# Retention in a two-layer language-model tower: on TensorE a tile's transposes are issued ahead of the scores of the tile four later

## What is computed

```python
gammas = 1.0 - exp(linspace(log(1/32), log(1/128), H))            # H = 8 heads of DH = 16
Dmat = gammas[:, None, None] ** abs(n[:, None] - n[None, :])      # 1024 x 1024 for each head
Q = _xpos(einsum('bsd,hde->bhse', X, W_Q), False)
K = _xpos(einsum('bsd,hde->bhse', X, W_K), True)
V = einsum('bsd,hde->bhse', X, W_V)
scores = einsum('bhse,bhte->bhst', Q, K)
p = softmax(scores, axis=-1) * Dmat[None]
Y = einsum('bhst,bhte->bhse', p, V)
...                                       # group norm of Y, gate with silu(X @ W_G)
return swish * Yn @ W_O
```

## Time and profile before

| | us |
|---|---|
| median of three executions | 3473.49 |
| lowest and highest of them | 3467.41 to 3475.9 |
| the profiled execution, its own time | 3499.97 |
| span of its profile | 3498.2 |
| first to last start of a tile's exponentials in it | 196.4 to 677.2 |

### The profile page before, as it was taken

One profiled execution on the slowest core, in us unless ns is written; L12 is line 12 of the kernel. 1 busy time (PEld: TensorE's weight loads), 2 busy tenths in 40 slices (PEclk: granted clock), 3 DMA queues, 4 the chain that ended last, 5 costly groups with the idle time before them and its releaser, 6 DMA issues.

```text
span 3498.2 us, 57433 instructions
## 1 busy us (share of the span) xinstructions
PE 3053.3 (87%) x18996; PEld 2673.3 (76%) x19032; DVE 2413.0 (69%) x4368; ACT 1801.3 (51%) x3135; POOL 1773.0 (51%) x1524
## 2 busy tenths in 40 slices
PE   1556666668999999879999999999799999999997
PEld 1434445457788888759999999999699999999986
DVE  1456766643677676657777777777577777777774
ACT  0256666523666565525555555555455555555544
POOL 5466656500200000126666666666366666666663
PEclk9879999969999999979999999999899999999997
DMA  1010000000000000010000000000000000000010
GB/s 41 32 25 18 19 13 18 7 25 21 13 0 0 0 0 0 11 50 28 27 27 27 27 27 27 27 27 28 17 28 27 27 27 27 27 27 27 27 34 7
DMA packets 36972, 75.92 MB, mean 22 GB/s; under 512 B 9644, under 2 KB 13876, under 8 KB 36120
## 3 DMA queue, kind: packets, MB, share of 16 engines
q1 hardware_dynamic: 35352, 71.68, 6.5%
q0 software_dynamic: 1536, 3.15, 0.3%
HBM read 65.36 MB, written 1.05 MB: 19 GB/s over the span
## 4 chain that ended last, share of the span: by engine, by line
PE 47%; issue 5%; POOL 3%; DVE 1%; ACT 0%; POOLq 0%; DVEq 0%; ACTq 0%
PE lat_ps_h L1837 19%; PE lat_ps_z L1851 9%; PE lat_ps_s L1763 7%; PE lat_ps_t L1790 6%; PE lat_ps_z L1781 3%; POOL lat_zz L1570 2%; PE lat_ps_z L1773 2%; PE lat_ps_z L1861 1%; POOL latm_wq L1549 0%; POOL latm_wq L1543 0%; POOL latm_att L1562 0%; POOL latm_vcg L1554 0%; PE lat_ps_s L1879 0%; DVE latm_norm L1669 0%; DVE latm_h L1675 0%
## 5 line engine op out<-in xcount | busy, mean ns | idle before, releaser
L1837 PE MATMUL lat_ps_h<-latm_share,latm_attT 100*128 100x256 f32 x6144 | 886.8, 286 | 0.1
L1837 PEld LDWEIGHTS lat_ps_h<-latm_share,latm_attT 100*128 100x128 f32 x6144 | 818.7, 189 | 24.9 <-DVE latm_attT L1626 11.8
L1562 POOL TENSOR_TENSOR latm_att<-latm_sc,latm_tot 128x400 f32<-128x400 f32 x516 | 441.3, 855 | 617.7 <-DVE latm_tot L1621 588.1
L1570 POOL TENSOR_TENSOR lat_zz<-lat_zz,lat_zsq 128x512 f32<-128x512 f32 x514 | 660.3, 1285 | 0.3
L1698 ACT ACTIVATE latm_sc<-latm_sc 128x400 f32<-128x400 f32 x516 | 279.1, 541 | 430.8 <-DVE latm_sc L1612 430.8
L1851 PE MATMUL lat_ps_z<-latm_attT,latm_vg 100*128 100x512 f32 x1536 | 485.8, 424 | 0.0
L1619 DVE TENSOR_REDUCE latm_tot<-latm_sc 128x4 f32<-128x400 f32 x516 | 291.3, 565 | 157.4 <-ACT latm_sc L1698 157.4
L533 POOL TENSOR_TENSOR ret_probs<-ret_probs,ret_shared 128x1024 f32<-128x1024 f32 x128 | 305.7, 2389 | 181.4 <-ACT ret_probs L666 181.4
L1626 DVE TENSOR_TENSOR latm_attT<-lat_ps_t,latm_attT 100x512 fp32r<-100x512 f32 x514 | 349.8, 681 | 61.7 <-ACT latm_attT L1714 61.7
L1714 ACT CAST latm_attT<-lat_ps_t 100x512 fp32r<-100x512 f32 x514 | 301.0, 586 | 147.3 <-PE lat_ps_t L1790 123.1
L1763 PE MATMUL lat_ps_s<-latm_wk,lat_xr 128*128 128x400 f32 x1548 | 368.8, 347 | 3.0 <-issue 3.0
(11 more groups left out here) (339 smaller groups left out, 5012.4 us busy)
## 6 DMA issues: line engine op xcount, KB each, us to landing
lat_w_in<-in_w_quads SPq DMA_DIRECT2D x65, 512.0 KB, 3.6
lat_wq_in<-in_wq_quads SPq DMA_DIRECT2D x65, 256.0 KB, 2.6
ret_qk_head<-ret_qk_parts SPq DMA_DIRECT2D x256, 32.0 KB, 2.0
moe_w<-in_W SPq DMA_DIRECT2D x2, 1024.0 KB
mha_wqk<-in_Wqk SPq DMA_DIRECT2D x1, 1152.0 KB, 5.6
ret_shared<-in_xpos_q SPq DMA_DIRECT2D x1, 1024.0 KB, 5.3
ret_shared<-in_xpos_k SPq DMA_DIRECT2D x1, 1024.0 KB, 5.0
latw_wkv<-in_Wkv SPq DMA_DIRECT2D x1, 1024.0 KB
```

The lines of the kernel that those rows point to most:

```text
L1562: nc.gpsimd.tensor_tensor(att[:, u].rearrange("p (j l) -> p j l", j=QH), sc[:, u].rearrange("p (j l) -> p j l", j=QH), tot[:, u].unsqueeze ...
L1570: nc.gpsimd.tensor_tensor(zz[:, t], zz[:, t], zsq[:, u], ALU.add).then_inc(s["zz_added"], 1)
L1837: mm = e.matmul(ps_h[:, t, :], attT[:, t % 2, a_part, j * P:(j + 1) * P], share[:, u, w_part, j * FF2:(j + 1) * FF2], start=False, stop=Fa ...
```

## The change

In PE's loop the two lines of `score(step + 2)` are moved from ahead of `extra(step)` to behind `turn(step - 2)`. Nothing is added or taken away, and the programs of the other engines stay as they are.

```diff
                 if LAG <= step < K + LAG:
                     gather(step)
-                if step + 2 < K:
-                    score(step + 2)
                 extra(step)
                 if 2 <= step <= K + 1:
                     turn(step - 2)
+                if step + 2 < K:
+                    score(step + 2)
```

## The result

The changed kernel takes 3336.69 us in the median (3334.86 to 3340.46) against 3470.45 for the kernel before in the same runs: a ratio of 0.9619, interval 0.9602 to 0.9637, or 134 us less. The forecast was 3370, with a range down to 3345.

The account below looks back on a forecast made before the run. A ring through ACT and PE was taken to bound the loop at 3.32 us a tile; 124.5 - 10 (norm) - 7 (ports) - 4 (half clock) = 103.5 us gained, from 3473.5 to 3370, range 3345 to 3405.

Parts of the forecast that it names:

- half clock: PE's scattered stretches at half clock, 37 us from 220 us on: 4 us charged, between 9 gained and 18 lost.
- the group norm and the ports: DVE's norm instructions no longer hidden, 10 us (3 to 13), and DVE waiting for POOL at SBUF, 7 us (0 to 10).
- The ring: Exponential, scores, transposes, two copies, next exponential: 1.28 + 0.44 + 0.64 + 0.96 = 3.32 us a tile, cut by the change.
- The steady tile: Loop over tiles: from 3.32 to 2.34 us, DVE's pace; 0.98 less, times 127 = 124.5 us.
- POOL and PE at its heels: Paces just below DVE's 2.34 us a tile: POOL 2.30 to 2.33, PE 2.24.
- Decay matrices kept whole: ACT's matrix, once in eight tiles, adds 1.79 us before and after; catching up, up to 27 us, put at nothing.
- Extra work at steps 10, 22 and 24 at nothing: PE's extra work stays ahead of the transposes and now also delays scores, which have a tile in hand: no cost.
- DMAs hidden: SP's work per head, about 8 us, stays hidden in a head of about 20.5, with some 12 us in hand.
- no change: Rival: something unseen, such as POOL's product, holds the transposes until the exponential's turn; 3473 us, chance 0.02.
- exclusion: Rival: POOL's product and DVE's subtractions cannot overlap; 3.54 us a tile, 28 us slower, 3502; chance 0.03.
- slower pace: Rival: PE idles at the waits for subtractions ahead of the scores; 2.75 us a tile, 3414 us, chance 0.13.

## Why the prediction was right or wrong

The gain was 30 us larger than the sum, and the time lies outside the range. The mechanism held, and three terms of the sum failed: half clock, charged with 4 us where it gave about 12; the group norm and the ports, charged with 17 us where they cost 3 to 6; and ACT's catching up behind the decay matrices, put at nothing because DVE "has no slack to recover", where it and the last hundredths of the pace gave about 10. The largest miss is the first.

- **The ring** of exponential, scores, transposes and copies: right; cutting half of it gave 2.83 for 2.84 us.
- **The steady tile** of 2.34 with DVE as the next bound: right, 2.33 measured, DVE without idle time in it and busy for 314.92 of 348.3 us of the loop. POOL and PE at its heels: PE yes (2.24), POOL with slack.
- **Decay matrices kept whole:** wrong. "DVE has no slack to recover" looked at DVE's pace and not at what it gets done while ACT is away. With the 0.44 caught up each time and the last hundredths of the pace, an undisturbed unit fell from 28.5 to 20.0 us, 8.5 where 8 x 0.98 = 7.84 was forecast. Over 127 steps that would be 135 us, not 124.5. Leaving the matrices out gave only 10 us in the loop, not 19, so the 1.36 us a matrix is shown for undisturbed units alone.
- **Group norm 10 and ports 7:** wrong in size; 3 to 6 together, by the two kernels without it, and none of it is a longer blocking of DVE at the ports (1.9 us, against 2.2 before).
- **Half clock, 4 against the change:** wrong in sign. The prediction let most of the stretches stay and priced them at the new pace; they went, from 64.7 us of half clock in the loop to 16.0. Counted step by step, it gave about 12 us. In the kernel before, the tiles at half clock behind the first 24 us took 9.7 us longer than the same tiles of that order at full clock (the 9 of the prediction), and about 2 us of that are left in the changed kernel. The four steps from tile 2 on gained 8.4 us where four ordinary ones gain 4.2, in the first 24 us, of which 23.7 were at half clock before and 9.2 are now. That the changed kernel's clock is high because PE stops for less time is argued, not tried by itself.
- **Extra work at steps 10, 22 and 24 at nothing:** wrong by about 4 us. These steps hang on `extra` in both kernels and gain less: the step behind tile 74 went from 6.17 to 5.77, so by 0.40 and not by 0.98. With the copies of the heads that ACT makes at steps 3 and 7 of a group (0.2 each) it is 4 us over the loop.
- **DMAs hidden, no change, exclusion, slower pace:** PE waited for `qk_head` once, for 17.4 us ahead of the first tile, as before; none of the rivals came.

Together: 135 - 6 (norm) - 4 (extra work) + 12 (clock) = 137, less about 4 at the ends of the loop, where the first two steps gain nothing and the last unit 5.8 us instead of 7.4: 133, and 132.5 were measured. The terms are read from single steps and good to 1 us or so each. The prediction took 103.5, since each open point was settled against the change, and its range put the clock and the norm at their best for 25 us only, with no room for the matrices.

## What to carry to other kernels

When an engine's program holds an instruction that waits for a fresh result ahead of one whose inputs are old, swap them; what it gives is the distance round the ring that is cut, down to the pace of the busiest engine, and both can be read from one tile's timeline. When the new pace is set by one engine, price the side work by who really waits: a stall on one engine lets the others run ahead, and they give some of it back. A PE that stops for a few us again and again may also pay in clock, so closing its gaps can give more than the gaps: here 12 of 132.5 us.

## What the hardware showed beyond this

With five extra matmuls in the retention block the instruction queue's share of the page changed from the first line (kernel before) to the second; with four it was the third:

```profile
q8 instruction: 49, 0.80, 0.1%
```

```profile
q8 instruction: 107, 1.75, 0.2%
```

```profile
q8 instruction: 53, 0.87, 0.1%
```

In the kernel with five, the latent block shows in each of seven passes of its first loop, about 120 us apart, two neighbouring tiles of 5.0 to 5.4 and 6.6 to 7.5 us, from one start of line 1769 to the next, where the median is 3.34. PE sits idle there with nothing that released it:

```profile
1677.83 0.81 PE L1769 MATMUL lat_ps_s<-latm_wk,lat_xr 128*128 128x400 f32 x3 [2.05 <-issue]
...
1680.78 2.29 PE L1843 MATMUL lat_ps_h<-latm_share,latm_attT 100*128 100x256 f32 x10 [1.90 <-issue]
```

The instruction queue from 1680 to 2480 us, most of this loop, in the kernel with five:

```profile
q8 instruction: 59, 0.97, 0.5%
```

In the same stretch the kernel before has no packet on that queue and the one with four has 1. The packets come some 9 in each pass, four of them within 12 us of the stall. So the number of instructions in one block slowed a loop in a later one, and, by that queue's packets, instructions were fetched anew in each pass of it. That the loop's code lies elsewhere, across some border, is argued: a program of another length did not have the stalls, but where the code lies was not looked at.
